# Nine of 24 convolutions moved from VectorE to ScalarE and TensorE in a scan-and-experts kernel

## What is computed

```python
xn = layernorm(x)
proj = xn @ W_in.T                       # 2 x 1024 channels
x, gate = proj[..., :1024], proj[..., 1024:]
for j in range(4): xc = xc + conv_w[:, j] * xpad[:, j:j + L, :]     # starts from conv_b
x = silu(xc)
ts, B, C = split(x @ W_x.T)              # 32 + 16 + 16, each RMS-normalised
dt = softplus(ts @ W_dt.T + b_dt)
state = state * exp(dt * A) + (dt * x) * B      # scan over time, 16 states per channel
y = sum_n(state * C) + x * D
s = (y * silu(gate)) @ W_out.T
out = x_in + s * silu(moe(xn))           # moe: top 2 of 8 experts, softmax weights
```

## Time and profile before

| | |
|---|---|
| median of 3 runs | 1090.31 us (1086.61 to 1090.49) |
| profiled execution: span from the first to the last instruction | 1086.8 us |
| DVE busy | 1022.8 us, 94% |
| POOL busy | 926.3 us, 85% |
| PE busy | 872.1 us, 80%, granted clock 0.91 of full speed |
| ACT busy | 733.8 us, 68% |

### The profile page before, as it was taken

How to read it: one execution, slowest core, us unless ns; L and a number is a source line. 1 busy time by engine, 2 the same in 40 slices (tenths; PEclk the granted TensorE clock), 3 DMA queues, 4 the chain that set the end, 5 groups by cost and what they waited for, 6 DMA issues and landing times.

```text
span 1086.8 us, 10255 instructions
## 1 busy us (share of the span) xinstructions
PE 872.1 (80%) x2774; PEld 323.8 (30%) x2774; DVE 1022.8 (94%) x1044; ACT 733.8 (68%) x1285; POOL 926.3 (85%) x365
## 2 busy tenths in 40 slices
PE   9944569798889998988656778989788997778576
PEld 5321123233223433333112223333223342223122
DVE  6779999999999999999999999899999999999998
ACT  3655567787787667766775667778767566676574
POOL 0629899999989889989889989798998978998995
PEclk9976788999989999999967879999999999799789
DMA  9355586556476665666743554766548566565714
GB/s 331 120 161 199 107 268 232 212 198 232 167 274 240 232 238 207 170 182 210 204 164 122 185 181 152 274 242 227 190 165 287 188 224 232 184 225 182 280 33 151
DMA packets 78089, 219.26 MB, mean 202 GB/s; under 512 B 15824, under 2 KB 17232, under 8 KB 71376
## 3 DMA queue, kind: packets, MB, share of 16 engines
q1 hardware_dynamic: 58096, 166.67, 44.7%
q10 hardware_dynamic: 12672, 31.46, 7.8%
q0 software_dynamic: 7264, 20.47, 6.9%
HBM read 176.85 MB, written 41.72 MB: 201 GB/s over the span
## 4 chain that ended last, share of the span: by engine, by line
DVE 36%; PE 22%; POOL 15%; issue 12%; DMA 9%; ACT 4%; SPq 2%; DVEq 0%; ACTq 0%; POOLq 0%
DVE sc_ps L1174 16%; POOL drive L567 10%; DVE drive L1174 6%; PE x_ps L1466 6%; DMA rep<-rep_rows 5%; DVE drive L1184 3%; PE f_ps L1419 3%; POOL drive L580 3%; PE y_ps L1434 3%; DMA x_slot<-xn_rows,slot_tok 2%; PE dt_ps L1394 2%; DVE x_ps L1113 2%; PE x_ps L1329 1%; PE x_ps L1351 1%; SPq L382 1%
## 5 line engine op out<-in xcount | busy, mean ns | idle before, releaser
L567 POOL TENSOR_TENSOR drive<-rep,b_all 128x2048 f32<-128x2048 f32 x127 | 575.8, 4538 | 44.1 <-DMA rep<-rep_rows 40.7
L799 ACT ACTIVATE sc_ps<-rep,a_neg 128x512 f32<-128x512 f32 x512 | 332.0, 681 | 86.2 <-DVE drive L1184 57.3
L1434 PE MATMUL y_ps<-drive,stack 128*32 128x512 f32 x1024 | 156.1, 687 | 89.7 <-DVE drive L1184 62.8
L1184 DVE TENSOR_TENSOR drive<-sc_ps,c_all 128x1024 f32<-128x1024 f32 x177 | 216.8, 1225 | 5.9
L1174 DVE TENSOR_TENSOR_SCAN sc_ps<-sc_ps,state,drive 128x512 f32<-128x512 f32 x178 | 218.4, 1273 | 3.8 <-ACT sc_ps L799 3.2
L1174 DVE TENSOR_TENSOR_SCAN sc_ps<-sc_ps,drive 128x512 f32<-128x512 f32 x176 | 205.3, 1212 | 5.5 <-ACT sc_ps L799 4.4
L580 POOL TENSOR_TENSOR drive<-drive,c_all 128x1024 f32<-128x1024 f32 x79 | 186.4, 2360 | 6.1 <-ACT state L778 6.1
L1419 PE MATMUL f_ps<-w_ring,xT_slot 128*128 128x512 f32 x368 | 176.5, 624 | 12.1 <-ACT xT_slot L811 12.1
L1394 PE MATMUL dt_ps<-xnT,w_g 128*128 128x512 f32 x232 | 117.8, 655 | 20.5 <-ACT dtu L766 20.4
L1419 PEld LDWEIGHTS f_ps<-w_ring,xT_slot 128*128 128x128 f32 x368 | 71.5, 201 | 118.3 <-issue 118.0
L1174 DVE TENSOR_TENSOR_SCAN drive<-sc_ps,state,drive 128x512 f32<-128x512 f32 x78 | 95.5, 1266 | 2.8 <-ACT sc_ps L799 2.8
(11 more groups left out here) (200 smaller groups left out, 1093.8 us busy)
## 6 DMA issues: line engine op xcount, KB each, us to landing
rep<-rep_rows SPq DMA_DIRECT2D x128, 512.0 KB, 6.7
w_ring<-wring SPq DMA_DIRECT2D x46, 1024.0 KB, 5.6
rep_rows<-dtu ACTq DMA_DIRECT2D x32, 512.0 KB, 3.3
slot_rows<-y_slot ACTq DMA_DIRECT2D x46, 256.0 KB
w_g<-wg_in SPq DMA_DIRECT2D x32, 256.0 KB, 2.7
w_x<-wx_in SPq DMA_DIRECT2D x24, 256.0 KB
xn_rows<-rep SPq DMA_DIRECT2D x16, 256.0 KB, 2.2
b_all<-bc_rows SPq DMA_DIRECT2D x16, 256.0 KB, 4.3
```

The lines of the kernel that those rows point to most:

```text
L567: pool.tensor_tensor(drive[:, m % RING, :, :], rep[:, n % 2, :, 1, :], b_all[:, q:q + 1, :].broadcast_to([P, NR, TC]), ALU.mult).then_inc( ...
L799: act.activation(sc[:, r, :], rep[:, n % 2, r, 0, :], ACT.Exp, scale=a_neg[:, lo:lo + 1]).then_inc(decay_ok, 1)
L1184: dve.tensor_tensor(drive[:, m % RING, 2 * h:2 * h + 2, :], sc[:, 2 * h:2 * h + 2, :], c_all[:, q:q + 1, :].broadcast_to([P, 2, TC]), ALU. ...
L1434: last = pe.matmul(y_ps[CH * r:CH * (r + 1), :], stack[:, :], drive[:, m % RING, r, :], start=False, stop=(m % NQ == NQ - 1))
```

## The change

For j >= 8 the x tiles 1, 3 and 5 of a chunk (three chunks, so nine convolutions) are no longer convolved by DVE. ACT's first tap stays in the bank, and PE adds the three others as matmuls with diagonal matrices of the weights, which SP loads from DRAM (a 128 x 384 block each, into the place of t_r). Silu then reads the bank. The wait for the bank is another: the late `next_x` waits for that Silu. In PE's order `sums(m+1)` now stands ahead of the late `next_x` and of `turn_slot` second, in all tiles. For n > 0 the skip term is written to `y_ps` by ACT (a Copy with the scale D, after the decays of m+1) and `sums` accumulate on it; `diagonal` is made once. In the nine `pe_log` tiles ACT's Relu is written in place in `dt_ps`, and PE adds three terms, not four. All nine x tiles are early ones, so `late_taps` is false everywhere and `take_x` does nothing.

```diff
+PE_TAPS = (1, 3, 5)
+def pe_taps(j):
+    return j >= NT and j % NT in PE_TAPS
...
+        taps = t_r[:, 0:(K - 1) * P].rearrange("p (k e) -> p k e", k=K - 1)
...
+        def x_bank_free(eng, j):
+            if late_taps(j - 1):
+                eng.wait_ge(x_took, took(j))
+            elif pe_taps(j - 1):
+                eng.wait_ge(x_ok, j)
+            else:
+                eng.wait_ge(conv_ok, dve_convs(j))
...
+            def load_taps(j):
+                if j is None or not pe_taps(j):
+                    return
+                if pe_convs(j):
+                    sp.wait_ge(taps_mm, pe_convs(j))
+                else:
+                    sp.wait_ge(lgT_mm, 1)
+                sp.dma_start(taps, taps_in[j % NT]).then_inc(s_tap, 16)
...
+                if early_x(c, t + 1) is not None:
+                    load_taps(NT * (c + 1) + early_x(c, t + 1))
...
             def silu_x(j):
                 c, t = divmod(j, NT)
-                act.wait_ge(conv_ok, j + 1)
-                act.activation(xy[:, c % 2, t, :], xy[:, c % 2, t, :], ACT.Silu).then_inc(x_ok, 1)
+                if late_taps(j):
+                    act.wait_ge(x_took, took(j + 1))
+                    rows = xy[:, c % 2, t, :]
+                elif pe_taps(j):
+                    act.wait_ge(taps_mm, pe_convs(j + 1))
+                    xy_free(act, c)
+                    rows = x_ps[:, :]
+                else:
+                    act.wait_ge(conv_ok, dve_convs(j + 1))
+                    rows = xy[:, c % 2, t, :]
+                act.activation(xy[:, c % 2, t, :], rows, ACT.Silu).then_inc(x_ok, 1)
...
-                    act.activation(t_r[:, :], dt_ps[:, :], ACT.Relu).then_inc(relu_ok, 1)
+                    act.activation(dt_ps[:, :], dt_ps[:, :], ACT.Relu).then_inc(relu_ok, 1)
...
+            def skip(n):
+                if n == 0:
+                    return
+                c, t = divmod(n, NT)
+                act.wait_ge(gated, n)
+                act.activation(y_ps[:, :], xy[:, c % 2, t, :], ACT.Copy, scale=dsk[:, t:t + 1]).then_inc(skip_ok, 1)
...
-                diagonal(n)
+                if n == 0:
+                    diagonal()
...
                 decays(m + 1, 1)
+                skip(n)
                 copy_slot_T(b, first_slot)
...
             def convolve(j):
                 c, t = divmod(j, NT)
+                if pe_taps(j):
+                    return
...
             def next_x(j):
-                pe.wait_ge(conv_ok, j)
+                x_bank_free(pe, j)
...
+            def add_taps(j):
+                if not pe_taps(j):
+                    return
+                pe.wait_ge(s_tap, 16 * pe_convs(j + 1))
+                pe.wait_ge(tap_ok, j + 1)
+                for k in range(1, K):
+                    last = pe.matmul(x_ps[:, :], taps[:, k - 1, :], x_pad[:, k:k + TC], start=False, stop=(k == K - 1),
+                                     skip_group_check=True)
+                last.then_inc(taps_mm, 1)
...
             def skip(n):
-                c, t = divmod(n, NT)
-                pe.wait_ge(diag_ok, n + 1)
                 if n:
-                    pe.wait_ge(gated, n)
-                pe.matmul(y_ps[:, :], diag[:, :], xy[:, c % 2, t, :], start=True, stop=False).then_inc(skip_mm, 1)
+                    pe.wait_ge(skip_ok, n)
+                    return
...
                 turn_slot(b, first_slot)
+                if early_x(c, t) is not None:
+                    add_taps(NT * (c + 1) + early_x(c, t))
                 skip(n)
...
                 expert(b, first_slot)
                 sums(m)
...
+                sums(m + 1)
                 if late is not None:
                     next_x(NT * (c + 1) + late)
                 turn_slot(b, second_slot)
-                sums(m + 1)
```

More of the change, by code:

```diff
@@ L51, with pe_convs, dve_convs, late_taps @@
 LATE_X = {2: 0, 3: 2, 4: 4, 5: 6}
+PE_TAPS = (1, 3, 5)
+def pe_taps(j):
+    return j >= NT and j % NT in PE_TAPS
+def pe_convs(k):
+    return sum(pe_taps(j) for j in range(k))
+def dve_convs(k):
+    return k - pe_convs(k)
+def late_taps(j):
+    return pe_taps(j) and j % NT in LATE_X.values()
+def took(k):
+    return sum(late_taps(j) for j in range(k))
 def act_turns(k):
@@ L481, in _ @@
                     load_expert(b, first_slot + 2)
+                if late_x(c, t) is not None and t > 2:
+                    load_taps(NT * (c + 1) + late_x(c, t))
                 if chunk_end:
@@ L490, in _ @@
                     load_expert(b, second_slot + 2)
+                if t == 1 and c < NCH - 1:
+                    load_taps(NT * (c + 1) + late_x(c, t + 1))
+                if early_x(c, t + 1) is not None:
+                    load_taps(NT * (c + 1) + early_x(c, t + 1))
                 if not even and t == NT - 1:
@@ L699, in copy_x @@
                 if kept > 0:
-                    act.wait_ge(conv_ok, kept)
+                    if pe_taps(kept - 1):
+                        act.wait_ge(taps_mm, pe_convs(kept))
+                    else:
+                        act.wait_ge(conv_ok, dve_convs(kept))
                     act.wait_ge(halo_ok, kept)
@@ L713, in silu_x, with take_x @@
                 c, t = divmod(j, NT)
-                act.wait_ge(conv_ok, j + 1)
-                act.activation(xy[:, c % 2, t, :], xy[:, c % 2, t, :], ACT.Silu).then_inc(x_ok, 1)
+                if late_taps(j):
[5 more added lines that the diff above has]
+                    rows = x_ps[:, :]
+                else:
+                    act.wait_ge(conv_ok, dve_convs(j + 1))
+                    rows = xy[:, c % 2, t, :]
+                act.activation(xy[:, c % 2, t, :], rows, ACT.Silu).then_inc(x_ok, 1)
+            def take_x(j):
+                if not late_taps(j):
+                    return
+                c, t = divmod(j, NT)
+                act.wait_ge(taps_mm, pe_convs(j + 1))
+                xy_free(act, c)
+                act.copy(xy[:, c % 2, t, :], x_ps[:, :]).then_inc(x_took, 1)
             act.wait_ge(ln_v, 1)
@@ L847, in keep_rows, with diagonal @@
                 act.dma_start(rep_rows[k % 2], dtu[:, :, :].rearrange("p k t -> p (k t)")).then_inc(s_dtu, 16)
-            def diagonal(n):
-                if n:
-                    act.wait_ge(skip_mm, n)
-                act.activation(diag[:, :], ident[:, :], ACT.Copy, scale=dsk[:, n % NT:n % NT + 1]).then_inc(diag_ok, 1)
+            def diagonal():
+                act.activation(diag[:, :], ident[:, :], ACT.Copy, scale=dsk[:, 0:1]).then_inc(diag_ok, 1)
+            def skip(n):
[4 more added lines that the diff above has]
+                act.activation(y_ps[:, :], xy[:, c % 2, t, :], ACT.Copy, scale=dsk[:, t:t + 1]).then_inc(skip_ok, 1)
             def silu_gate(n):
@@ L1423, in skip @@
             def skip(n):
[L1424 to L1425 removed]
                 if n:
[L1427 to L1428 removed]
+                    pe.wait_ge(skip_ok, n)
+                    return
+                pe.wait_ge(diag_ok, 1)
+                pe.matmul(y_ps[:, :], diag[:, :], xy[:, 0, 0, :], start=True, stop=False)
             def sums(m):
@@ L1434, in sums @@
                     last = pe.matmul(y_ps[CH * r:CH * (r + 1), :], stack[:, :], drive[:, m % RING, r, :],
-                                     start=False, stop=(m % NQ == NQ - 1))
+                                     start=False, stop=(m % NQ == NQ - 1), skip_group_check=m >= NQ)
                 last.then_inc(sum_ok, 1)
@@ L1590 @@
     gate_w[:, :E] = v["gate_w"]
+    taps = np.zeros((NT, P, K - 1, P), f)
+    for k in range(1, K):
+        taps[:, np.arange(P), k - 1, np.arange(P)] = v["conv_w"].reshape(NT, P, K)[:, :, k]
     consts = np.ones((P, CONSTS), f)
@@ L1607 @@
         "gate_w": gate_w.reshape(HK, P, CH).transpose(1, 0, 2),
+        "taps_in": taps,
         "means": mean_w,
```

27 lines of the change are left out of this document (15 added, 12 removed).

## The result

The changed kernel takes 1129.8 us, the median of four runs (1124.6 to 1131.9), against 1089.4 us before: a ratio of 1.036, with an interval of 1.033 to 1.040. The prediction was slower, 1107 us with 1080 to 1121; the direction held, but 1129.8 lies above the range: 17.7 us more were forecast and 40.4 came. The profiled execution has a span of 1126.0 us, 39.2 more than before, where 18.6 had been added up.

What follows compares the result with a forecast made beforehand. DVE was taken to bound the touched tiles, 98% busy, with POOL and PE close behind. Delays of the late convolution in six odd tiles summed to 18.6 us, 1086.8 + 18.6 = 1105.4, so 1107 us was forecast, range 1080 to 1121.

Steps and rivals of the forecast that it cites:

- The new chain: POOL's low product, `sums(m+1)`, projection, ACT's copy, first tap: 6.2 us before DVE's late convolution can start; chance 0.56.
- a second loop of this kind: Even tiles: a loop like that tying POOL to DVE's dt through `rep` in odd tiles; not added to the sum.
- the prediction's own formula: Delay of a tile with a late x: low product's end + 6.2 us - start of DVE's late convolution before.
- The odd tiles: Tiles 3, 5, 11, 13, 19, 21: delays of 2.4, 3.0, 0.9, 5.9, 3.6 and 2.8 us, sum 18.6.
- the delays of a chunk add: Tile 3's delay passes over dt, `rep` and POOL to tile 5: 18.6 us summed, 12.5 if only the largest counts.
- The low clock: Rival: PE slows down after standing still ahead of `sums(m+1)`, 2.45 us more in six chains, about 1120 us; chance 0.10.
- The gain kept by DVE: Rival: POOL's low product ends early enough, so DVE's 20.2 us of removed convolutions are saved, about 1070 us; chance 0.18.
- The 1.7 us of taps beyond the skip matmul: PE ahead of first expert and `sums(m)`: 2.8 us of taps replace 1.1 of skip; delay covered by POOL's low product.
- POOL's idle time: 2.7 us in a touched tile, cited for the rival in which POOL's low product starts sooner.
- the pause of PE ahead of `sums(m+1)`: Tile 3: 1.4 us after PE's work ends at 189.9, used against the rival of a slower PE clock.
- scatter: The 3.5 us by which the median of the runs stood above the span of 1086.8 us before.

Runs made afterwards that it cites:

- e1: Kernel after, with the late projection and the second slot's turn ahead of `sums(m+1)` on PE again, as in the kernel before: 1094.6 us, ratio 1.007.
- e2: Kernel before with only the order on PE changed, `sums(m+1)` ahead of the late projection and the second turn: 1137.1 us, ratio 1.044.
- e6: Kernel after with the late projection back ahead of `sums(m+1)` and only the second slot's turn left behind it: 1099.0 us, ratio 1.010.
- e17: Kernel after with the new PE order left only in the six tiles t = 3, 5, the old order in t = 2, 4: 1110.0 us, ratio 1.020.
- e18: Kernel after with the new PE order left only in the six tiles t = 2, 4, the old order in t = 3, 5: 1110.0 us, ratio 1.018.
- e5: Kernel after with the old PE order in the three tiles t = 2 alone: 1122.0 us, ratio 1.032.
- e3: Kernel before, its PE order kept, with the nine convolutions on PE and Relu in place, but the skip term by PE as before: 1099.0 us, ratio 1.008.
- e8: e1 with ACT, in the nine tiles, copying the tapped x out and doing decays(m+2, 1) ahead of its table load and Silus: 1096.6 us, ratio 1.009.
- e7: e1 with one tap matmul instead of three in the nine tiles: 1090.6 us, ratio 1.002.
- e16: e15 with two of the late projection's four matmuls also left out in the nine tiles: 1082.7 us, ratio 0.994.
- e15: e1 with plain copies for Silus, no Silu table loads and one tap matmul instead of three in the nine tiles: 1089.8 us, ratio 1.000.

## Why the prediction was half right

**The new chain** was right, and so was its price: 6.2 us forecast, 6.3 in tile 3. e1, e2 and e6 show that the projection behind `sums(m+1)` is the loss.

**The step that failed** is the sentence "The even tiles have a second loop of this kind, beside the first, which I don't add". Odd tiles were held to give the whole delay; in truth each tile's DVE work follows the last, and a wait in an even tile delays the next odd one. So a term of some 20 us was put at nothing: the even tiles grew by 21.0 us in the kernel after, and e17 and e18 show the two halves, each 21.4 us over before. The working was at hand. These are POOL's low product m+1 and DVE's late convolution in tiles 2, 4, 10, 12, 18 and 20 of the kernel before:

```profile
158.31 2.36 POOL L580 TENSOR_TENSOR drive<-drive,c_all 128x1024 f32<-128x1024 f32 x1
160.48 1.54 DVE L1113 SCALAR_TENSOR_TENSOR x_ps<-x_pad,cw,x_ps 128x512 f32<-128x512 f32 x2
...
218.36 2.38 POOL L580 TENSOR_TENSOR drive<-drive,c_all 128x1024 f32<-128x1024 f32 x1
...
227.21 1.54 DVE L1113 SCALAR_TENSOR_TENSOR x_ps<-x_pad,cw,x_ps 128x512 f32<-128x512 f32 x2
...
400.63 2.35 POOL L580 TENSOR_TENSOR drive<-drive,c_all 128x1024 f32<-128x1024 f32 x1
...
405.44 1.55 DVE L1113 SCALAR_TENSOR_TENSOR x_ps<-x_pad,cw,x_ps 128x512 f32<-128x512 f32 x2 [0.91 <-ACT x_ps L708]
...
463.45 2.35 POOL L580 TENSOR_TENSOR drive<-drive,c_all 128x1024 f32<-128x1024 f32 x1
469.44 1.54 DVE L1113 SCALAR_TENSOR_TENSOR x_ps<-x_pad,cw,x_ps 128x512 f32<-128x512 f32 x2
...
661.04 2.36 POOL L580 TENSOR_TENSOR drive<-drive,c_all 128x1024 f32<-128x1024 f32 x1
...
666.37 1.54 DVE L1113 SCALAR_TENSOR_TENSOR x_ps<-x_pad,cw,x_ps 128x512 f32<-128x512 f32 x2
...
725.20 2.37 POOL L580 TENSOR_TENSOR drive<-drive,c_all 128x1024 f32<-128x1024 f32 x1
...
732.32 1.54 DVE L1113 SCALAR_TENSOR_TENSOR x_ps<-x_pad,cw,x_ps 128x512 f32<-128x512 f32 x2
```

By the prediction's own formula (low product's end + 6.2 - start of the convolution) they give 6.4 - 0.3 + 3.7 + 2.6 + 3.2 + 1.5 = 17.1 us; measured were 21.0. With the 18.6 of the odd ones the span comes to 1122.5, against 1126.0. That is worked out afterwards, and the total agrees better than its parts. To the tiles t = 2 (2, 10 and 18) the formula gives 13.3 of the 17.1, but e5, which takes out their waits, is only 6 to 8 us shorter; in tile 3 the forecast was 2.4 and the tile grew by 0.3.

**The odd tiles**: 18.6 forecast, 16.1 in the kernel after, where the even ones before them have taken part of it, and 22.4 in e17, where they stand alone. That the delays of a chunk add was right.

**The low clock** was a rival for the odd tiles (1120), with 0.10 for it, and part of it came, mostly in even ones. In tile 2, the granted clock from 164.8 us on is 0.60, near the lower of the two levels (1.2 of 2.4 GHz), behind a wait of 5.3 us; `sums` and projection take 1.93 + 5.77 us there, against 1.06 + 3.70 in tile 3, 2.9 us more. Tile 2's convolution starts 25.7 us after `gate_tile`, 12.2 before; the 13.5 more are 6.4 by the formula, some 3.0 by the clock and 4.1 because the low product itself is later. The late projections of tiles 12, 13 and 18 are slow as well:

```profile
488.54 5.24 PE L1408 MATMUL x_ps<-xnT,w_x 128*128 128x512 f32 x8
...
526.73 4.92 PE L1408 MATMUL x_ps<-xnT,w_x 128*128 128x512 f32 x8
...
693.00 5.40 PE L1408 MATMUL x_ps<-xnT,w_x 128*128 128x512 f32 x8
```

The granted clock in them is 0.70, 0.75 and 0.68, behind waits for POOL's low product of 2.85, 3.42 and 3.54 us. Together the four projections take 6.5 us more than at 3.70 each. The formula at 6.2 us a chain has none of this, so that it came within 3.5 us of the span is in part luck.

**The gain kept by DVE** (1070) was ruled out for the wrong reason. The prediction held that a removed convolution is worth its full time as long as nothing takes over within about 3 us, and put its loss on the new order alone. e1 and e3 show no gain in the old order either. Engine averages (28.5 us of PE in a tile of 32.2) hide that PE's series up to the late x was only 1.0 us ahead of DVE in tile 5, with next to no wait in it from the second expert of tile 4 on. The 1.7 us of taps beyond the skip matmul, costed at nothing beyond what POOL covers, were on that path.

**The decays** weren't in the prediction: DVE's waits for them rose from 10.4 to 26.9 us. e8, without them in the nine tiles, isn't faster than e1: they are the same stall seen at an earlier instruction.

**Three readings** of the prediction were off and changed little. POOL's idle time is 32.2 - 29.2 = 3.0 us a tile by the earlier trace rows, not 2.7. And the pause of PE ahead of `sums(m+1)` in tile 3, put at 1.4 us, left out that `sums(m)` takes 1.06 of it; measured were 0.82. Of the 3.5 us between the span and the median, called scatter, some 2 us lie between span and time in every execution on record.

**Left open**: what single late events have in e7 to e16 beside the tiles t = 4, and tile 2, whose low product comes 4.1 us later in the kernel after, and which takes 37.3 us in e1, 31.9 in e6 and 32.5 in the kernel before.

## What to carry to other kernels

Sum a delay over every tile in which the moved wait occurs, not over those whose work changes: engines that queue in order pass each tile's wait to the next. Before work moves from the busiest engine to the third, compare their series up to the point where one hands over to the other, not their shares: here PE reached the late x only 1.0 us ahead of DVE, where the page's 80% promised 20% of the span. If leaving out work on the receiving engine shortens the tile one for one, as in tile 5 from e8 to e15 to e16, that engine's series has become the bound in this order, even where the traces blame waits on another.
